# The end of a fused attention and router kernel: the seventh tile's attention output turned by TensorE instead of by DMA, its output products placed between the last weighings

## What is computed

```
x = x + tanh(g_xattn[0]) * fake_quant_matmul(layernorm(x), ctx_4096)
x = x + tanh(g_ffn[0])   * (base linear layer + low-rank Fourier update)(layernorm(x))
x = x + tanh(g_xattn[1]) * attention(layernorm(x), ctx_4096; Wq, Wk, Wv, Wo)     # 16 heads of 96, 4 key heads
x = x + tanh(g_ffn[1])   * router_mix(layernorm(x))

# attention:   softmax(q k^T / sqrt(96)) v for each head, then  out @ Wo.T
# router_mix:  scores = softmax(h @ router_weight.T + router_bias)   (64 experts)
#              keep the 8 largest;  out = h * sum(kept) + kept @ expert_bias
```

## Time and profile before

| | |
|---|---|
| median of 3 runs | 1095.9 us (1095.38 to 1097.76) |
| the profiled execution | 1099.59 us, of which the span 1097.7 us |
| TensorE busy | 1043.4 us (95%) |
| VectorE, ScalarE, GpSimd busy | 618.7, 620.1, 644.9 us |
| granted TensorE clock, mean | 0.982 |

### The profile page before, as it was taken

One profiled execution on the slowest core, in us unless ns is written; L12 is line 12 of the kernel. 1 busy time (PEld: TensorE's weight loads), 2 busy tenths in 40 slices (PEclk: granted clock), 3 DMA queues, 4 the chain that ended last, 5 costly groups with the idle time before them and its releaser, 6 DMA issues.

```text
span 1097.7 us, 18325 instructions
## 1 busy us (share of the span) xinstructions
PE 1043.4 (95%) x7207; PEld 586.4 (53%) x7207; DVE 618.7 (56%) x1067; ACT 620.1 (56%) x687; POOL 644.9 (59%) x349
## 2 busy tenths in 40 slices
PE   8969999999999989999999999999999999989875
PEld 3535544444544555556566655656655655655542
DVE  6866949653223455545545554654654654666656
ACT  5656635432123577656666755656755566667733
POOL 4358678332000588656668845667865567677841
PEclk9979999999999999999999999999999999989996
DMA  9777664753223999999999999999999999999993
GB/s 339 251 233 210 203 221 125 163 96 58 70 92 102 199 205 207 202 207 183 198 179 212 198 198 185 182 201 197 189 206 199 173 209 180 165 168 179 181 170 115
DMA packets 522281, 198.94 MB, mean 181 GB/s; under 512 B 487684, under 2 KB 502916, under 8 KB 522196
## 3 DMA queue, kind: packets, MB, share of 16 engines
q1 hardware_dynamic: 522196, 197.78, 87.2%
HBM read 56.88 MB, written 13.63 MB: 64 GB/s over the span
## 4 chain that ended last, share of the span: by engine, by line
PE 77%; SPq 7%; DMA 6%; DVE 4%; POOL 2%; ACT 2%; issue 1%; POOLq 0%; DVEq 0%; ACTq 0%
PE ps L560 30%; PE ps L796 17%; PE ps L770 9%; PE ps L811 9%; PE ps L813 5%; DMA region_o<-region_y 3%; PE ps L697 3%; SPq L522 2%; SPq L520 2%; POOL region_y L1699 2%; PE ps L582 2%; DMA v_scratch<-region_o 1%; SPq L499 1%; DVE p_max L1535 1%; DMA region_c<-region_b 1%
## 5 line engine op out<-in xcount | busy, mean ns | idle before, releaser
L1699 POOL TENSOR_TENSOR region_y<-p,region_b 128x1536 f16<-128x1536 f32 x128 | 396.9, 3101 | 287.6 <-ACT region_b L1238 225.4
L1535 DVE TENSOR_REDUCE p_max<-ps 128x1 f32<-128x1536 f32 x128 | 224.9, 1757 | 130.5 <-PE ps L796 130.5
L1228 ACT ACTIVATE p<-ps,p_max 128x1536 f32<-128x1536 f32 x128 | 197.0, 1539 | 172.9 <-DVE p_max L1535 172.9
L796 PE MATMUL ps<-region_q,region_c 96*128 96x512 f16 x1152 | 270.1, 379 | 0.8 <-DMA region_c<-region_q 0.8
L1238 ACT ACTIVATE region_b<-ps,p_max 128x1536 f16<-128x1536 f32 x128 | 196.6, 1536 | 66.0 <-DMA region_c<-region_b 66.0
L811 PE MATMUL ps<-region_q,region_c 128*128 128x192 f16 x1536 | 209.1, 247 | 16.5 <-DMA region_o<-region_y 11.9
L813 PE MATMUL ps<-region_q,region_o 128*128 128x96 f16 x1536 | 203.8, 207 | 0.0
L811 PEld LDWEIGHTS ps<-region_q,region_c 128*128 128x128 f16 x1536 | 150.7, 98 | 37.9 <-issue 18.5
L796 PEld LDWEIGHTS ps<-region_q,region_c 96*128 96x128 f16 x1152 | 105.4, 98 | 109.0 <-issue 1.4
L813 PEld LDWEIGHTS ps<-region_q,region_o 128*128 128x128 f16 x1536 | 150.8, 98 | 12.2 <-issue 0.3
L560 PE MATMUL ps<-region_w,region_q 128*128 128x512 f16 x576 | 136.0, 382 | 3.9 <-POOL region_w L1699 2.4
(11 more groups left out here) (147 smaller groups left out, 1108.4 us busy)
## 6 DMA issues: line engine op xcount, KB each, us to landing
stage<-ctx_in SPq DMA_DIRECT2D x16, 512.0 KB, 4.9
stage<-ctx_t_in SPq DMA_DIRECT2D x15, 512.0 KB, 7.4
stage<-wq_in SPq DMA_DIRECT2D x16, 384.0 KB, 4.1
stage<-wo_in SPq DMA_DIRECT2D x16, 384.0 KB, 4.4
k_scratch<-region_o SPq DMA_DIRECT2D x12, 384.0 KB, 5.8
region_q<-k_scratch SPq DMA_DIRECT2D x8, 576.0 KB, 5.8
region_q<-v_scratch SPq DMA_DIRECT2D x8, 576.0 KB, 6.5
x_res<-x_in SPq DMA_DIRECT2D x8, 512.0 KB, 10.0
```

Of the source, the lines that this page charges most:

```text
L796: ins = nc.tensor.matmul(bank(NSB * (m % 2) + sb_), q_head[0:HD, b, h, hq, qt * P:(qt + 1) * P], k_head[0:HD, b, hk, sb_ * 512:(sb_ + 1) * ...
L1228: nc.scalar.activation(p32[:, m % 2, :], rows, ACT.Exp, bias=p_max[:, m % 4:m % 4 + 1], accum_out=den[:, m % 4:m % 4 + 1]).then_inc(e32_ok, 1)
L1535: nc.vector.reduce_max(p_max[:, m % 4:m % 4 + 1], rows, axis=AX, negate=True).then_inc(max_ok, 1)
L1699: return nc.gpsimd.tensor_tensor(out, a, b, op)
```

## The change

The turning of group 30 moves from the DMA way to TensorE. SyncE's `turn_o` of it, ScalarE's `take_o` and GpSimd's `take_low_o` of it go. TensorE gains three float32 transposes (`turn_last(0, 30, ...)`, into PSUM bank 0), ScalarE and VectorE one copy and one subtraction of 128x384. The output products 60 and 61 go to banks 1 and 2 and are issued ahead of and behind the weighing of unit 126; products 62 and 63 go to banks 0 and 3, the turning of tile 4's weights (`expert_turn(5, 4)`) between them, and `expert_mix(7, 3, 1)` behind them. On VectorE `choose(4, 4)`, `add_out(1, 60)` and `add_out(2, 61)` move ahead, and `add_mix(7, 3, 1)` behind both statistics. On ScalarE `expert_norm(6)` moves behind the weights and the scaling of tile 4.

```diff
@@ sync
-            turn_o(o_at(NU - 1))
             turn4(5)
             store(2)
             turn4(6)
@@ tensor
-            weigh(NU - 3)
+            pe.wait_ge(exp_ok, NU - 1)
+            pe.wait_ge(o_ok, NU - 4)
+            turn_last(0, 30, (0, 1, 2))
             pe.wait_ge(fin_ok, 5)
             expert_mix(7, 2, 1)
+            weigh(NU - 3)
+            pe.wait_ge(lt_lo, 1)
+            out_last(1, 30, 0, (0, 1, 2))
+            out_last(2, 30, 1, (0, 1))
             weigh(NU - 2)
+            out_last(2, 30, 1, (2,))
             pe.wait_ge(exp_ok, NU)
             expert_mix(5, 3, 0)
             pe.wait_ge(o_ok, NU - 1)
-            turn_last((0, 1))
+            turn_last(4, 31, (0, 1))
             weigh(NU - 1)
+            pe.wait_ge(lt_lo, 2)
+            out_last(0, 31, 0, (0, 1))
+            pe.wait_ge(o_ok, NU)
+            turn_last(4, 31, (2,))
+            pe.wait_ge(fin_ok, 7)
+            expert_turn(5, 4)
+            out_last(3, 31, 1, (0, 1))
+            pe.wait_ge(lt_lo, 3)
+            out_last(0, 31, 0, (2,))
+            out_last(3, 31, 1, (2,))
             pe.wait_ge(fin_ok, 6)
             expert_mix(7, 3, 1)
-            pe.wait_ge(lt_lo, 1)
-            out_last(2, 0, (0, 1))
-            out_last(3, 1, (0, 1))
-            pe.wait_ge(o_ok, NU)
-            turn_last((2,))
-            out_product(0, 60)
-            out_product(1, 61)
-            pe.wait_ge(lt_lo, 2)
-            out_last(2, 0, (2,))
-            out_last(3, 1, (2,))
-            pe.wait_ge(fin_ok, 7)
-            expert_turn(5, 4)
             pe.wait_ge(wx_ok, 5)
             router(5, 5)
@@ scalar
-                if o_at(m) is not None:
+                if o_at(m) is not None and m < NU - 1:
                     take_o(o_at(m))
...
+            take_last(1, 0, 30, slice(0, 3))
             expert_norm(5)
-            take_last(slice(0, 2))
-            take_last(slice(2, 3))
-            expert_norm(6)
+            take_last(2, 4, 31, slice(0, 2))
+            take_last(3, 4, 31, slice(2, 3))
             expert_weights(5, 4)
             expert_scale(4)
+            expert_norm(6)
             expert_exp(5)
@@ vector
+            take_low_last(1, 0, 30, slice(0, 3))
             invert(NU - 3)
             take_out(NU - 3)
             add_mix(7, 2, 1)
+            choose(4, 4)
+            add_out(1, 60)
             invert(NU - 2)
             take_out(NU - 2)
+            add_out(2, 61)
             add_mix(5, 3, 0)
-            take_low_last(slice(0, 2))
+            take_low_last(2, 4, 31, slice(0, 2))
             invert(NU - 1)
             take_out(NU - 1)
-            take_low_last(slice(2, 3))
-            add_mix(7, 3, 1)
-            choose(4, 4)
-            add_out(0, 60)
-            add_out(1, 61)
+            take_low_last(3, 4, 31, slice(2, 3))
             expert_stats(6)
-            add_out(2, 62)
+            add_out(0, 62)
             add_out(3, 63)
             expert_stats(7)
+            add_mix(7, 3, 1)
             logits(5, 5)
             choose(5, 5)
```

More of the change, by code:

```diff
@@ L893, in _, with turn_last, out_last @@
                     weigh(m - LAG)
-            def turn_last(js):
+            def turn_last(at, k, js):
                 for j in js:
-                    ins = nc.tensor.transpose(bank(4)[:, j * P:(j + 1) * P], o_tok[:, 1, j * P:(j + 1) * P], ident[:, :])
+                    ins = nc.tensor.transpose(bank(at)[:, j * P:(j + 1) * P], o_tok[:, k % 2, j * P:(j + 1) * P],
+                                              ident[:, :])
                 ins.then_inc(lt_ready, 1)
-            def out_last(at, half, js):
+            def out_last(at, k, half, js):
                 for j in js:
-                    ins = passes(bank(at), split_passes(lambda h: o_t[:, 1, h, j, :],
+                    ins = passes(bank(at), split_passes(lambda h: o_t[:, k % 2, h, j, :],
                                                         lambda h: wo[:, h, j, half * 512:(half + 1) * 512]),
@@ L938, in _ @@
             for half in range(2):
-                pe.wait_ge(wo_free, 61 + half)
+                pe.wait_ge(wo_free, 63 - half)
                 pe.wait_ge(y7_ok, half + 1)
@@ L1252, in _, with take_last @@
                     expert_scale(SCALE_X[last])
[L1254 to L1258, removed]
+            def take_last(n, at, k, js):
+                act.wait_ge(lt_ready, n)
+                act.wait_ge(wo_ready, 2 * k - 2)
+                copy(o_t[:, k % 2, HI, js, :], bank(at)[:, js.start * P:js.stop * P].rearrange("p (j q) -> p j q", q=P)
                      ).then_inc(lt_hi, 1)
+            take_last(1, 0, 30, slice(0, 3))
             expert_norm(5)
-            take_last(slice(0, 2))
-            take_last(slice(2, 3))
-            expert_norm(6)
+            take_last(2, 4, 31, slice(0, 2))
+            take_last(3, 4, 31, slice(2, 3))
             expert_weights(5, 4)
             expert_scale(4)
+            expert_norm(6)
             expert_exp(5)
@@ L1648, in _, with take_low_last @@
                     expert_stats(STATS4[last])
[L1650 to L1653, removed]
+            def take_low_last(n, at, k, js):
+                dve.wait_ge(lt_hi, n)
+                minus(o_t[:, k % 2, LO, js, :], bank(at)[:, js.start * P:js.stop * P].rearrange("p (j q) -> p j q", q=P),
+                      o_t[:, k % 2, HI, js, :]).then_inc(lt_lo, 1)
+            take_low_last(1, 0, 30, slice(0, 3))
             invert(NU - 3)
```

## The result

| | before | changed |
|---|---|---|
| median of 8 runs each, us | 1097.53 (1095.38 to 1103.66) | 1092.48 (1089.61 to 1094.85) |
| ratio to before | | 0.9943, interval 0.9922 to 0.9964 |
| span of the profiled execution, us | 1097.7 | 1087.5 |

The changed kernel is faster by 0.57%, 6.3 us (3.9 to 8.6 by the interval). The ratio is not the quotient of the two medians, which is 0.9954 (5.05 us) and lies inside the interval. The further runs of before put its median 1.6 us above the three that the forecast started from; the ratio, applied to those (1095.9), gives 1089.7, beside a forecast of 1088.8. The measured median itself, 1092.48, lies 0.9 us above the range that I gave (1086.3 to 1091.6): the size of the gain was forecast well, the absolute time less so, since it started from three runs of before.

What follows compares the result with a forecast made beforehand. It took the end to be bound by unit 127's DMA transposes, then one long chain behind its weighing. Gains of 6.9 to 7.5 us, less 0.1, were taken as 7.1 off 1095.9: 1088.8 us, range 1086.3 to 1091.6.

Steps and rivals of the forecast that it cites:

- Products 60 and 61 hidden in the waits: Around unit 126's weighing: 18 matmuls, 3.9 us, hidden in waits of 2.38 and 0.94 us and the mix's old place.
- SyncE, ScalarE, GpSimd at 0: Removing group 30's two DMA transposes, a cast and a subtraction gains 0, since nothing of the chain waited for them.
- The 0.1 for the transfer of unit 127: Tile 5's transposes, now queued behind unit 127's transfer, could slow it; taken as 0.1 us.
- Its bound of +1.5 us: Upper bound on slowing unit 127's transfer: it took 4.12 us, the longest of its line 5.6.
- The main term, 6.1 us: Behind unit 127: statistics of tile 6 start at 1063.15, not 1069.26, so expert_norm(6) starts 6.1 us earlier, at 1066.05.
- The other branch: VectorE's remaining work through tile 5's choice ends at 1071.9; tile 7's transposes then end 6.9 us earlier at half clock.
- the lower of my two cases: Tile 7's transposes at half clock, 6.9 us gained; the other case, full clock, gains about 7.4.
- My sign of being wrong: One of three signs: a chain reaching tile 7's transposes over tile 5's choice instead of tile 6's norm.
- The collision of VectorE and GpSimd: Tile 5's choice against GpSimd's low half of tile 6: 0.4 us apart, counted 0, at most 2.1 us if colliding.
- rival a: Gain of only 2.2 to 6 us: unit 127's transfer 1.5 late, the choice colliding for 2.1, or both partly; chance 0.09.
- rivals b and c: b: clock stays full, even at the end, 1086.0, chance 0.06; c: clock falls at 1052.6, slower, 1097.5, chance 0.03.
- Rival b's case: Larger gain: shorter TensorE pauses keep its clock full, even at the end; about 2.8 us more, 1086.0; chance 0.06.

Runs made afterwards that it cites:

- e10: Kernel with products 60 and 61 late (e2), plus 12 matmuls that nothing reads in TensorE's wait for unit 126; 38.4 us from issue to end, ratio 0.9965.
- e2: Changed kernel with products 60 and 61 issued behind the last turning, their additions behind the last low half; 41.4 us from issue to end, ratio 0.9994.
- e3: Changed kernel with group 30's old cast, low half and DMA transposes kept as a load, result unread; 34.9 us from issue to end, ratio 0.9939.
- e1: Kernel before with VectorE's new order alone (choose(4, 4) earlier, add_mix(7, 3, 1) later); 42.2 us from issue to end, ratio 1.0003.
- e11: Kernel before with 22, 8 and 10 matmuls that nothing reads in three late TensorE waits; 39.2 us from issue to end, ratio 0.9974.
- e7: Changed kernel with 11, 5 and 10 matmuls that nothing reads in three late TensorE waits; 32.3 us from issue to end, ratio 0.9940.
- e9: Changed kernel with e6's earlier statistics and transposes and e7's matmuls that nothing reads together; 31.8 us from issue to end, ratio 0.9890.
- e4: Changed kernel with choose(4, 4) back behind the last low half and expert_turn(5, 4) behind the products; 35.1 us from issue to end, ratio 0.9949.
- e8: Changed kernel with group 30's first low half queued later on VectorE, behind choose(4, 4); 38.1 us from issue to end, ratio 0.9977.
- e5: Changed kernel with VectorE's statistics of tile 6 ahead of the last low half; 34.5 us from issue to end, ratio 0.9937.
- e6: As e5, plus tile 7's first four transposes issued ahead of expert_turn(4, 5); 34.0 us from issue to end, ratio 0.9934.

## Why the prediction was right

The direction, the place and the size were right: 7.1 us forecast, 6.3 in the times, 7.7 in the profile. Step by step, each time counted from the weighing of unit 127:

- *Products 60 and 61 hidden in the waits*: right. The low half ended at 1049.62, the last matmul of unit 125's weighing began at 1049.62, and the products began at 1049.68; the new wait cost 0. TensorE was free at 1056.14, 0.78 us before unit 127 (I had said half a us). e10 shows what they cost outside: 4.2 us, as I had written for e2.
- *SyncE, ScalarE, GpSimd at 0*: right, by e3. The 0.1 for the transfer of unit 127 was 0.01. Its bound of +1.5 us was too narrow, though: the longest of 5.6 us in the earlier trace rows is of the line's last four transposes only. Over all 128 of before they took 3.7 to 7.6 us. At unit 127 the thirteen profiles show 3.6 to 4.2 us.
- *The main term, 6.1 us*: the statistics of tile 6 came after 3.62 us (forecast 3.71), `expert_norm(6)` after 6.51 (forecast 6.61), 6.2 us earlier than before.
- *The other branch*: tile 5's choice was done after 12.2 us (forecast 12.5), the transposes began after 12.81 (forecast 12.8) at half clock, `router(7)` came after 16.25 (forecast 16.2 to 16.3 for half clock): 6.9 us, the lower of my two cases. My sign of being wrong, a chain over tile 5's choice, stayed away by little: the transposes waited 0.25 us for tile 7's norm behind `expert_turn(4, 5)`, which had waited for the choice.
- *What I left out*: from `router(7)` to the end 14.3 us against 15.1. 0.17 us is the clock, which rose one mix earlier; 0.36 lies between the last choice and the last addition, where the chain of before had 0.40 us of issue ahead of the addition that after has not; 0.23 is the last store. None of these was tested; that they are scatter is a guess.
- *The collision of VectorE and GpSimd* (rival a): it did not come up. GpSimd's low half of tile 6 ended at 1067.96, the choice's first subtraction began at 1068.23, 0.27 us apart where I had written 0.4. The subtraction did run beside a short GpSimd instruction, and took 0.22 us there as before (1078.10, GpSimd idle):

```profile
1067.92 0.55 POOL L1705 TENSOR_TENSOR rstd<-var_c,mhalf 128x1 f32<-128x1 f32 x1
```

  I wrote that no run shows such a collision. That is so for the end alone. At its head the trace of before has VectorE subtractions with two SBUF inputs beside long GpSimd ones, and there they wait (rows in the last section), as the Trainium skill has it (SBUF — State Buffer, Who interferes with whom). So the rival had a ground in the trace that I had. Whether the choice, run into the low half, would have cost the 2.1 us was not tried.
- *The clock* (rivals b and c): here my reasons were thin. I said that the clock had held through the old waits of before, and counted nothing for it. e1, e2 and e11 show it falling there (0.57, 0.66 and 0.50, 0.53 in their windows). So the changed kernel, which fills that wait, also protects the weighings that follow (no fall there in the changed kernel, e3 to e7 and e9); in the pair of profiles before and after this is not seen, since before happened to keep its clock. With the old order the fall cost only 0.3 us (e1, e11); in e2 it cost 2.0. How often it falls in before I can't say: e1 and e11 have the same waits as before, and in both it did. Rival b's case came in full only with fillers; e4 and e8 had about 1.5 us of it by themselves.

## What to carry to other kernels

Look for the work that stands between the last thing that must be waited for and the chain that ends the kernel, and ask of each piece whether its inputs were there before that wait. Moving 18 matmuls from behind the last transfer into the waits ahead of it gave 4.2 us, more than half of the gain, and the choice that it freed VectorE to do early gave 1.7 (e4). The remaining 1.0 us up to `router(7)` and 0.8 behind it were not taken apart by an experiment. A kernel whose runs start their tail up to 6 us apart is read from an event inside it that the change hardly moves, and a profile at one clock level is not to be compared with one at the other before the difference is taken out.

## What the runs showed of the hardware

TensorE's clock moved the end of these kernels by 1.5 to 3.3 us without any change in the work that counts. It showed two levels, 1.00 and 0.50 of 2.4 GHz, as the Trainium skill has it (TensorE: Matmul & The Clock Gate, What's actually happening). Ahead of or at unit 126 it fell behind a wait of 2.33 us (e1), 2.35 (e11), 2.93 (e2) and 3.69 (e8), and did not behind one of 2.38 (before). Further on, it fell behind waits of 2.21 us (e5, e6) and 2.51 (changed), too. Whether such a wait costs clock was thus not the same from one execution to the next. Matmuls that nothing reads, placed in the waits, held it at 1.00 in e7, e9, e10 and e11 through every stretch that they covered, and where they were short enough to be over before the awaited semaphore they delayed nothing. In e9 five of them put off tile 7's first transposes by 0.3 us against e6 (11.89 and 11.56 us behind the weighing of 127); that was covered by VectorE, which came to the first low half of them after 13.4 us in both.

A VectorE subtraction that reads two tensors in SBUF was held up by a GpSimd subtraction that reads SBUF. Rows of before at its head:

```profile
9.22 0.96 DVE L1290 TENSOR_TENSOR region_w<-region_q,region_w 128x768 f16<-128x768 f32 x1 [1.01 <-ACT region_w L969]
...
10.94 2.13 POOL L1699 TENSOR_TENSOR region_c<-stage,region_c 128x1024 f16<-128x1024 f32 x1 [3.14 <-ACT region_c L969]
...
11.78 2.11 DVE L1290 TENSOR_TENSOR region_w<-region_q,region_w 128x768 f16<-128x768 f32 x1 [1.60 <-ACT region_w L969]
```

With GpSimd idle it took 0.96 us. The next one began while GpSimd was at work until 13.07 and took 2.11, ending 0.82 behind it. Two more, also beside GpSimd, took 2.6 and 2.9.
